# An attention and FFN kernel on one core: the first block's four mixing tiles, the low-rank weights, three rounds of weight sums and the bias add change their places

## The reference, cut to what matters

```
h  = mix_w[token_type] applied to each sequence   # 64x64 over the tokens ("mix")
q, k, v = h @ Wq.T, h @ Wk.T, h @ Wv.T            # 32 heads of q, 8 of k and v, width 128
q, k = rmsnorm(q), rmsnorm(k)                     # with gains
x1 = x + attention(q, k, v, causal, ALiBi) @ Wo.T
y  = x1 @ W2.T + b2 + scale * lora_b(lora_a(x1))  # low-rank part by adapter of the sequence
out = x1 + y @ W_base.T + b_base + SCALING * fourier(masked low-rank of y)
```

## Time and profile before

| what | value |
|---|---|
| median of 3 runs | 2399.7 us (2398.89 to 2400.05) |
| the profiled execution's own time | 2400.53 us |
| its span | 2398.7 us |
| PE busy | 2368.9 us, 99% of the span |
| DVE, ACT, POOL busy | 1750.3 us (73%), 1330.4 us (55%), 280.5 us (12%) |
| DMA | 316 MB, 132 GB/s on average |

### The profile page before, as it was taken

One profiled execution on the slowest core, in us unless ns is written; L12 is line 12 of the kernel. 1 busy time (PEld: TensorE's weight loads), 2 busy tenths in 40 slices (PEclk: granted clock), 3 DMA queues, 4 the chain that ended last, 5 costly groups with the idle time before them and its releaser, 6 DMA issues.

```text
span 2398.7 us, 32788 instructions
## 1 busy us (share of the span) xinstructions
PE 2368.9 (99%) x11578; PEld 1967.4 (82%) x11578; DVE 1750.3 (73%) x2866; ACT 1330.4 (55%) x3305; POOL 280.5 (12%) x336
## 2 busy tenths in 40 slices
PE   8989999999999999999999999999999999999998
PEld 6878888888888888888888888888888888888886
DVE  6768878686847867777856777777876686868682
ACT  4246656566625656566724656565744565657560
POOL 0222010101111001010011101010011101010110
PEclk9999999999999999999999999999999999999999
DMA  7765434441542242423343242423244242424250
GB/s 258 257 256 199 154 134 148 140 149 63 188 145 92 88 139 76 141 79 129 134 156 118 71 158 71 158 71 123 97 170 148 77 147 69 153 77 141 70 194 35
DMA packets 88436, 316.12 MB, mean 132 GB/s; under 512 B 12716, under 2 KB 13228, under 8 KB 87124
## 3 DMA queue, kind: packets, MB, share of 16 engines
q1 hardware_dynamic: 70292, 247.14, 30.5%
q0 software_dynamic: 16256, 62.92, 7.2%
q10 hardware_dynamic: 1728, 3.98, 0.5%
HBM read 282.54 MB, written 31.46 MB: 131 GB/s over the span
## 4 chain that ended last, share of the span: by engine, by line
PE 94%; DVE 4%; issue 1%; DMA 1%; ACT 0%; POOL 0%; ACTq 0%; POOLq 0%; DVEq 0%
PE main L1019 79%; PE pv_bank L1215 4%; PE qt_bank L1180 3%; PE s_bank L1196 2%; PE s_bank L1197 2%; PE pt_bank L1204 1%; PE pt_bank L1019 1%; DVE ring L1480 1%; DVE act_lo L1480 0%; DVE act_lo L1483 0%; DVE setup L1480 0%; PE qt_bank L1117 0%; PE s_bank L1117 0%; DMA mask<-in_masks 0%; DMA t_scratch<-sums 0%
## 5 line engine op out<-in xcount | busy, mean ns | idle before, releaser
L1019 PE MATMUL main<-ring,act_hi 128*128 128x512 f32 x3584 | 1149.2, 402 | 0.1
L1019 PEld LDWEIGHTS main<-ring,act_hi 128*128 128x128 f32 x3584 | 641.3, 189 | 112.7 <-issue 2.1
L1019 PE MATMUL main<-ring,act_lo 128*128 128x512 f32 x1792 | 702.5, 392 | 0.0
L1019 PE MATMUL main<-ring,lefts 128*128 128x512 f32 x2688 | 624.3, 391 | 0.0
L1480 DVE TENSOR_TENSOR ring<-raw,ring 128x1024 fp32r<-128x1024 f32 x448 | 554.4, 1240 | 59.5 <-ACT ring L1226 58.0
L1019 PEld LDWEIGHTS main<-ring,lefts 128*128 128x128 f32 x2688 | 501.7, 188 | 103.0
L1226 ACT ACTIVATE ring<-raw 128x1024 fp32r<-128x1024 f32 x448 | 472.5, 1057 | 180.8 <-PE main L1019 163.6
L1019 PEld LDWEIGHTS main<-ring,act_lo 128*128 128x128 f32 x1792 | 336.8, 188 | 74.6
L1816 POOL TENSOR_TENSOR rstd<-mean,half 128x4 f32<-128x4 f32 (+1 forms) x192 | 174.7, 910 | 1568.5 <-DVE mean L1605 1568.3
L1385 ACT ACTIVATE prob<-score,peak 128x64 f32<-128x64 f32 x512 | 136.7, 338 | 157.3 <-DVE peak L1660 156.8
L1357 ACT ACTIVATE sq<-main 128x128 f32<-128x128 f32 x640 | 168.8, 277 | 70.7 <-PE main L1019 68.4
(11 more groups left out here) (172 smaller groups left out, 2390.4 us busy)
## 6 DMA issues: line engine op xcount, KB each, us to landing
raw<-in_wq SPq DMA_DIRECT2D x128, 512.0 KB, 4.0
raw<-t_scratch SPq DMA_DIRECT2D x128, 512.0 KB, 3.3
raw<-in_wo SPq DMA_DIRECT2D x96, 512.0 KB, 3.3
raw<-in_wkv SPq DMA_DIRECT2D x64, 512.0 KB, 4.1
sums<-in_wo POOLq DMA_DIRECT2D x32, 512.0 KB, 6.6
t_scratch<-sums POOLq DMA_DIRECT2D x32, 512.0 KB, 4.2
raw<-f_scratch SPq DMA_DIRECT2D x32, 512.0 KB, 5.5
acc<-in_x POOLq DMA_DIRECT2D x16, 512.0 KB, 3.7
```

The source lines that it names most:

```text
L1019: mm = eng.matmul(bank, a, b, start=start and n == 0 and m == 0, stop=stop and n == len(terms) - 1 and m == 2, skip_group_check=further)
```

## The change

1. `mix(0, 0)` moves from behind product (8, 0) to between products (7, 0) and (7, 1); `mix(0, 1)` from behind product (8, 1) to ahead of product (8, 0).
2. `split_mix(0, 2)` moves ahead of product (8, 0), and so ahead of `beff_hi(0)` and of every chunk, on ACT and DVE. `mix(0, 2)` moves from behind kv step 0 to ahead of it, between chunk 4 and chunk 5. `split_mix(0, 3)` comes behind chunk 5, and `mix(0, 3)` between kv steps 0 and 1 (before: between 1 and 2).
3. The load of `lora_a` and its split come behind all six chunks.
4. The first three rounds of sums in block 0 are placed at quarters 4.5, 20 and 35.5 instead of 0.5, 17 and 33.5.
5. `biased_x` of both tiles of a pair is placed behind the second tile's splits, and waits for the second tile's last `a_lo` instead of its own `x1_t`. This holds in all four blocks.

```
-ROUND_AT = (0.5, 17, 33.5, 104, 180)
+ROUND_AT = (4.5, 20, 35.5, 104, 180)
...
+            if n == KT - 1:
+                self.mix(0, 0)
             self.product(n, 1)
...
         self.add("x2", 0)
         self.add("x3", 0)
+        self.mix(0, 1)
+        self.split_mix(0, 2)
         self.product(KT, 0)
+        for i in range(UNIT_CHUNKS):
+            self.prepare(both=True)
+        self.product(KT, 1)
         self.prepare(both=True)
-        self.mix(0, 0)
+        self.mix(0, 2)
         self.prepare(both=True)
-        self.prepare(both=True)
-        self.split_mix(0, 2)
-        self.prepare(both=True)
+        self.split_mix(0, 3)
         self.load(("lora_a",), ("loraa_lo", ()))
         self.add("loraa_hi")
         self.add("loraa_lo")
-        self.product(KT, 1)
-        self.mix(0, 1)
-        self.prepare(both=True)
-        self.prepare(both=True)
         self.add("fx_store")
...
-            if k == 0:
-                self.split_mix(0, 3)
-            if k in (1, 2):
-                self.mix(0, k + 1)
+            if k == 1:
+                self.mix(0, 3)
...
-        self.add("biased_x", blk, t)
+
+        if t % 2 == 1:
+            for half in (t - 1, t):
+                self.add("biased_x", blk, half)
...
                 elif stage == "biased_x":
                     blk, t = key
-                    w.wait_ge("x1_t", blk, t, 1)
+                    w.wait_ge("a_lo", "x1", blk, t | 1, 1)
```

## The result

The changed kernel takes 2403.93 us (median of 22 runs, 2402.1 to 2407.26), the kernel before 2400.41 us on the same chip (22 runs, 2398.89 to 2402.8). The ratio is 1.0014, with a 95% interval of 1.0008 to 1.0021: slower by 3.5 us, or 0.14%. The forecast was 2396.4, faster by 3.3, with a range up to 2400.5: the time lies 3.4 us above it, and the kernel became slower where it was to become faster. The difference is small, under the 0.2% (4.8 us) that the prediction calls about what can be told from no change, but the interval leaves out "no change at all". In all that follows, one run of one version (2619.72 us at a granted clock of 0.849) is left out. The profiled execution has a span of 2402.0 us, 3.3 more than before.

A forecast was written before the change was run, and what follows sets the result against it. The prediction took PE to bound the kernel, busy for 2368.9 of 2398.7 us. Its terms, 0.9 - 1.1 - 3.6 + 0.5 = -3.3 us, on the median of 2399.7 gave 2396.4 us, with an 8-in-10 range of 2390.5 to 2400.5.

The forecast's parts named there:

- the chain ahead of mix(0, 3): Late x2, then chunk 4 and the splits queued behind it, leave PE idle 8.15 us before mix(0, 3).
- chunk 4 early: Rival: chunk 4 lands after 3.4 us, PE idles 2.5 us less; -5.8 us, 2393.9 us; chance 0.22.
- the boundary closes: Rival: the wait for chunk 4 never reaches PE; -13.1 us, 2386.6 us; chance 0.08.
- the block-0 gain fails: Rival: at block 0's end another DVE instruction is late by as much; +0.3 us, 2400.0 us; chance 0.12.
- the estimate of 4.4 us: Chunk 4's load latency from 2.0 us fixed and half of 436 GB/s; set aside for the trace's 5.9 us.
- 8.15 + 1.65: Ahead of mix(0, 3): 8.15 us of PE idleness, plus 1.65 us lost to the halved clock behind it.
- the account of losses of this stretch: From product (8,0) done to kv step 2: 10.8 us lost instead of 9.9, so +0.9 us.
- Rounds of sums. -1.1 us.: Later rounds in block 0 let key_t(0) and key_t(1) find inputs ready: -1.1 us; bounds -0.9 more, or +2.
- biased_x at block 0's end, -3.6: Block 0's end: w_lo no longer waits for POOL's addition, a_lo comes 2.1 us earlier; -3.6 us, bounds 0 and -3.95.
- Blocks 1 to 3, +0.5: Block ends: POOL's two additions hold up low_lo, costing 0.1 to 0.3 us per block; +0.5 us, bounds 0 and 9.
- POOL first: Rival: in blocks 1 to 3 POOL precedes w_lo, shutting DVE out for both additions; +5.4 us, 2405.1 us; chance 0.08.

The follow-up runs named there:

- the rounds alone: The kernel before with only block 0's first three rounds of sums moved to quarters 4.5, 20 and 35.5: 2402.96 us, ratio 1.0012.
- the bias addition alone: The kernel before with only biased_x of both tiles placed behind the second tile's splits: 2398.03 us, ratio 0.9992.

## Why the prediction was wrong

**Right: the chain ahead of mix(0, 3).** x2 is late by the mix ahead of the last copy, `x_hi` of tile 2 waits for it (134.98, forecast 134.45), mix(0, 2) waits 1.06 (forecast 1.0), and mix(0, 3) stands behind chunk 4, eight splits, w_lo(5) and x_lo(0, 3). Moving only the chunks took 7 us of the wait away. The rivals "chunk 4 early", "the boundary closes" and "the block-0 gain fails" did not happen. Chunk 4 took 7.4 us beside a round of sums and 5.4 without it. The Trainium skill, DMA: Bandwidth & Descriptors, section Queues, rings and completion order, has each DMA engine take turns between the queues; the estimate of 4.4 us made from that page was too low for either.

**Mis-sized: "8.15 + 1.65".** Chunk 4 was taken at 5.9 us of latency and took 7.4, which makes 9.37 of the 8.15. The latency's upper bound, 7.9, had held it. The row of the kernel before was a weak guide: there the round's loads were issued from 134.5 to 136.0, 2.7 us ahead of chunk 4; now they are issued from 136.7 to 138.2, 0.9 us ahead of it, so that more of the round lies beside the chunk. The clock's loss of 1.65, taken from an idleness of 3.54 us, was 3.3: up to kv step 2 there are 10.79 us from the start of mix(0, 3) for 7.5 of work. The granted clock stays at 0.50 until about 161.1, 6.7 us after PE starts again. In five other versions with idleness of 7.4 to 10.0 us here it came back after 4.3 to 5.1 us, and their loss up to key_t(0) was about 2 where it was 3.0 here. So some 1.0 of the excess of 1.65 seems to belong to the profiled execution. The 1.65 itself was one execution's value: behind a wait of 3.5 us at key_t(0), the way from it to key_t(1), less the wait at its end, took 7.8 us with the rounds alone (the clock stayed at 1.00), 9.4 in the kernel before and 10.4 with the bias addition alone. Together the account of losses of this stretch went from 9.9 to 14.3 us, +4.4 where +0.9 was forecast.

**The failed step: "Rounds of sums. -1.1 us."** The wait at key_t(1) did go, but not by the rounds: with the new order and the old rounds no key transpose waits, so parts 1 to 3 bring that gain, and the one at key_t(3) with it. The step had named two causes, the additions and "a mix in step 2", and gave their 1.1 to the rounds. What it missed is the price of the later rounds. It was put at nothing, with an upper bound of +2 for POOL's queue; between key_t(1) and 245 us the changed kernel takes 3.2 us more than the kernel before and 4.0 more than the same kernel with the old rounds; the ratios of these two are 3.6 us apart. Part 4 alone, in the old order, costs 3.3 us in the same stretch. The two queues have a share each. A third of the 3.2 (1.1) is what the prediction named and then let stand: `rstd` behind the loads of quarter 20, on an in-order queue that waits for landings. Most of the rest lies at waits of another kind, which it did not name (1.0 at key_t(3), 0.58 and 0.60 at query transposes, 0.97 at a score product): additions of 1.2 us among norms and chunk splits, where DVE has no pause, and at key_t(3) also `rstd` held for 1.1 us beside a `w_lo`. That these are DVE's is read from its packed timeline and from their staying when the loads are moved. No run moved the additions alone, so this part is argued.

**Right: biased_x at block 0's end, -3.6.** The two traces give -3.65 there, alone it gave a median 2.6 lower, and with the new order and the old rounds 3.4 lower. That the number fits to 0.05 is in part luck: 2.2 of it is the wait, the rest the clock, and with the rounds alone the clock stayed at 1.00 behind the same wait of 2.4 us, so that an execution without this loss has less to win. **Blocks 1 to 3, +0.5:** +0.4 by the number, but only 0.16 of it lies where it was forecast, at block 1's end (3.04 at its last `x1_t`, 1222.78, against 2.88 at its first). Within the ends of blocks 2 and 3 nothing is lost, and where the rest comes from stays open. The rival "POOL first" had the order right for blocks 2 and 3 and the price wrong: POOL does get in first there, but the w_lo of 3.42 us waits for one addition, not for both, and PE waits for nothing. The rule of the Trainium skill, SBUF — State Buffer, section Who interferes with whom, that the first to issue keeps the port for its instruction, agrees with the 3.42 as the wait for one addition; the prediction had stretched it over two instructions.

The sum by its terms, forecast and in the traces: stretch +0.9 and +4.4; rounds -1.1 and +1.8 (-1.4 up to key_t(1), +3.2 behind it); block 0's end -3.6 and -3.65; later blocks +0.5 and +0.4. That is -3.3 and +3.0; the 0.34 by which the profiled execution is late ahead of it all gives the 3.3 of the spans.

## What to carry to other kernels

When two parts of a change could each remove the same wait, ask of each what it costs when the other has left nothing to win: here the later rounds cost about 4 us for a wait that the new order alone removes. An item that waits for a DMA should stand in no engine's queue ahead of what TensorE wants next: two chunks put behind the tile's split and the low-rank weights behind the first norm, together with the old rounds and the later bias addition, made the kernel 0.34% faster than before, with the same work. But place them by what they share the DMA with: the same items, put behind still further beside a 2 MB store and a round of sums, gave the gain away again as a wait of 5.27 us. And a loss of clock that one profile shows is a weak term for a sum: the same wait cost between nothing and about 2.7 us in three executions here.

## What the runs showed of the hardware that was not expected

- Behind an idleness of 7.4 to 10.0 us of PE the granted clock stayed at 0.50 for 4.3 to 6.7 us of work in kernels with nearly the same instructions there, and cost between about 1.9 and 3.0 us up to key_t(0). Behind a wait of 3.5 us at key_t(0) it was at 0.50 for 3.5 us of work in one kernel and 5.9 in another, and stayed at 1.00 in a third. Behind one of 2.4 us ahead of mix(0, 3) it fell in four versions and not in a fifth. So one profile's value of it is uncertain by more than a microsecond.
- VectorE, held by a GpSimd addition of two SBUF operands, gets in between two such additions that are recorded as adjacent (3.42 us for a w_lo that takes 1.22; POOL's pair stretched from 4.73 to 5.73).
- The latency of 512 KB weight loads: 5.4 us for chunk 4 without a round of sums beside it, 6.9 to 8.1 with one issued just ahead of it (5.9 in the kernel before, where it was issued earlier), 11 to 14 for later chunks beside a round and a 2 MB store.
